# Router bias on TensorE, logits compared in place, expert numbers of the tiles counted among seven

## The reference

```python
xn = layernorm(x)                      # x: 16 x 256 x 128, 4096 tokens in 32 tiles of 128
s = attention(xn)                      # 16 heads of 8, LoRA on q, k, v, ALiBi, causal
logits = xn @ Wr + br                  # 8 experts
indices = argmax(softmax(logits))
for i in range(8):                     # a token not routed to i enters expert i as zeros
    h = relu((xn * (indices == i)) @ W1[i] + b1[i])
    f = f + (h @ W2[i] + b2[i])
out = x + s * silu(f)
```

## Time and profile before

| | us |
|---|---|
| median of 3 runs | 296.31 |
| lowest, highest | 295.81, 296.85 |
| the profiled execution: its own time | 296.07 |
| its span, first to last instruction | 294.2 |
| outside the span | 1.87 |
| PE busy | 267.8 (91%) |
| DVE busy | 228.1 (78%) |
| ACT busy | 185.5 (63%) |
| POOL busy | 152.6 (52%) |

### The profile page before, as it was taken

How to read it: one execution, slowest core, us unless ns; L and a number is a source line. 1 busy time by engine, 2 the same in 40 slices (tenths; PEclk the granted TensorE clock), 3 DMA queues, 4 the chain that set the end, 5 groups by cost and what they waited for, 6 DMA issues and landing times.

```text
span 294.2 us, 12787 instructions
## 1 busy us (share of the span) xinstructions
PE 267.8 (91%) x5196; PEld 203.6 (69%) x5196; DVE 228.1 (78%) x483; ACT 185.5 (63%) x331; POOL 152.6 (52%) x226
## 2 busy tenths in 40 slices
PE   7899999684996999999999999999999999979962
PEld 3556555353674788888887888888788888856641
DVE  3788999789987578596868768685875868676996
ACT  3335355444466668777777778777776876558960
POOL 3073293115436577866677667667766533343100
PEclk9999999979999799999999999999999999999997
DMA  4799556687415442332425433231524623108553
GB/s 137 207 240 212 127 166 194 203 240 225 112 36 134 109 126 67 95 97 57 108 55 129 123 101 84 74 91 51 133 51 96 147 54 90 30 29 250 138 163 111
DMA packets 50970, 35.98 MB, mean 122 GB/s; under 512 B 5112, under 2 KB 48376, under 8 KB 50784
## 3 DMA queue, kind: packets, MB, share of 16 engines
q1 hardware_dynamic: 46680, 28.89, 37.0%
q0 software_dynamic: 2496, 5.12, 7.0%
q10 hardware_dynamic: 1736, 1.15, 1.6%
HBM read 15.28 MB, written 6.75 MB: 75 GB/s over the span
## 4 chain that ended last, share of the span: by engine, by line
PE 68%; DVE 18%; issue 6%; DMA 3%; POOL 2%; SPq 1%; ACT 1%; ACTq 0%; DVEq 0%; POOLq 0%
PE bank L1359 14%; PE bank L1367 12%; PE bank L1273 11%; PE bank L1324 10%; PE bank L1183 4%; DVE row_max L812 4%; PE bank L1281 3%; PE bank L1343 3%; PE bank L1253 2%; PE bank L1190 2%; DVE xn_all L1063 2%; PE bank L1351 2%; DVE w_slots L977 2%; DVE xn_all L1057 1%; DVE o_turned L1020 1%
## 5 line engine op out<-in xcount | busy, mean ns | idle before, releaser
L812 DVE TENSOR_REDUCE row_max<-bank 128x2 f32<-128x512 f32 (+3 forms) x176 | 105.6, 627 | 19.2 <-PE bank L1261 16.3
L757 ACT ACTIVATE probs<-bank 128x512 f32<-128x512 f32 (+1 forms) x176 | 89.5, 558 | 46.4 <-PE bank L1281 46.1
L1273 PE MATMUL bank<-qk_stack 64*64 64x64 bf16 (+3 forms) x1024 | 60.8, 237 | 6.5 <-ACT probs L757 3.3
L1253 PE MATMUL bank<-qk_stack 64*64 64x64 bf16 (+3 forms) x1024 | 61.7, 237 | 1.1 <-DMA qk_stack<-parts 0.7
L554 POOL DMA_INDIRECT expert_rows<-y_slot,token_of x39 | 38.6, 990 | 37.2 <-PE bank L1359 22.8
L532 POOL DMA_INDIRECT xs_slot<-normalised_rows,from_row x39 | 39.7, 1018 | 24.9 <-PE bank L1281 17.9
L1273 PEld LDWEIGHTS bank<-qk_stack 64*64 64x64 bf16 x1024 | 34.3, 108 | 23.6 <-issue 10.7
L739 ACT ACTIVATE w_slots<-w_all 128x1156 f32 x39 | 45.5, 1167 | 4.0 <-issue 3.4
L1324 PE MATMUL bank<-probs,v_diag 128*32 128x64 f32 (+3 forms) x1024 | 46.5, 311 | 1.2 <-issue 1.0
L1045 DVE TENSOR_TENSOR hT<-bank,w_slots 128x512 f32<-128x512 f32 x39 | 27.0, 691 | 23.3 <-PE bank L1359 23.3
L1359 PE MATMUL bank<-xsT_slot,w_slots 128*128 128x128 f32 x312 | 44.6, 286 | 0.2 <-issue 0.2
(11 more groups left out here) (132 smaller groups left out, 346.1 us busy)
## 6 DMA issues: line engine op xcount, KB each, us to landing
qk_stack<-parts SPq DMA_DIRECT2D x120, 64.0 KB, 2.1
qk_stack<-parts SPq DMA_DIRECT2D x32, 128.0 KB, 2.8
w_all<-w_experts SPq DMA_DIRECT2D x8, 512.0 KB, 4.6
x_all<-x SPq DMA_DIRECT2D x7, 512.0 KB, 5.2
normalised_rows<-xn_all SPq DMA_DIRECT2D x4, 512.0 KB, 5.2
xn_all<-expert_rows SPq DMA_DIRECT2D x8, 256.0 KB, 5.2
out<-xn_all SPq DMA_DIRECT2D x7, 256.0 KB, 3.2
xs_slot<-normalised_rows,from_row POOLq DMA_INDIRECT x39, 3.2
```

Source lines behind the costliest of these rows:

```text
L757: act.activation(probs[:, m % PROBS, 0:w], bank[:, 0:w], ACT.Exp).then_inc(emptied, 1)
L812: dve.tensor_reduce(row_max[b % 2][:, n, pairs[0]:pairs[-1] + 1], bank[:, 0:ln_u * len(pairs)].rearrange("p (c k) -> p c k", k=ln_u), AX.X ...
L1253: pe.matmul(bank[to, c * ln_u:(c + 1) * ln_u], q[rows, p, n * BLK:(n + 1) * BLK], k[rows, p, 0:(n + 1) * BLK], start=(c == 0), stop=False, ...
L1273: pe.matmul(bank[rows, c * ln_u:(c + 1) * ln_u], k[rows, p, kb * BLK:(kb + 1) * BLK], q[rows, p, kb * BLK:], start=(c == 0), stop=False, s ...
```

## The change

The bias travels in row 0 of 32 more columns of the array that holds the dense weights (`dense`, 288 KB where it was 272), and its own DMA goes. Behind the four logits matmuls of each `route` PE issues four more, with one row of weights (the bias) and a row of ones as data, 256 columns each, into the same PSUM columns. The wait for the constants moves from DVE to PE. `keep_logits` is the transposition alone; its target is now a part of `xsT_slot`, a buffer not yet in use, with room for all 32 tiles, and `choose` reads 8 of each 32 columns there. The tile's expert number is the count over seven totals, which needs no limit; DVE ends with the sum, and POOL converts it behind `fill_v` at (2, 4).

```diff
-        dense = sb("dense", [P, 4 * P + 32])
+        dense = sb("dense", [P, 4 * P + 64])
+        br_sb = dense[0:1, 4 * P + 32:4 * P + 64]
-        br_sb = sb("br_sb", [P, E])
-        te_cmp = sb("te_cmp", [1, SLOT_TILES, E])
+        te_cmp = sb("te_cmp", [1, SLOT_TILES, E - 1])
+        logits_turned = xsT_slot[:, :, :, :].rearrange("p r j k -> p (r j k)").rearrange("p (n e) -> p n e", e=32)
+        logits = logits_turned[:, :, 0:E]
...
+            def keep_tile_experts():
+                pool.wait_ge(S["tile_sums_done"], 1)
+                pool.tensor_copy(tile_expert[:, :], te_f[:, :]).then_inc(S["tile_expert_done"], 1)
...
                     if i + 1 < NB and g == FILL_V:
                         fill_v(i + 1)
+                    if (i, g) == TILE_EXPERTS_AT:
+                        keep_tile_experts()
...
-            act.dma_start(br_sb[:, :], br.partition_broadcast(P)).then_inc(S["br_in"], 16)
...
-                dve.transpose(logits_turned[:, :, :].rearrange("p n e -> p (n e)"), bank[:, 0:ROUTE_TILES * 32]).then_inc(emptied, 1)
-                wait_vec_emptied(dve, "logits", r)
-                if r == 0:
-                    dve.wait_ge(S["br_in"], 16)
-                    dve.wait_ge(S["constants_in"], 16)
-                dve.tensor_tensor(logits[:, tiles, :], logits_turned[:, :, 0:E],
-                                  br_sb[:, :].unsqueeze(1).to_broadcast([P, ROUTE_TILES, E]), ALU.add).then_inc(S["logits_turned_done"], 1)
+                dve.transpose(logits_turned[:, tiles, :].rearrange("p n e -> p (n e)"), bank[:, 0:ROUTE_TILES * 32]).then_inc(emptied, 1)
...
-                dve.wait_ge(S["logits_turned_done"], ROUTES)
+                for r in range(ROUTES):
+                    wait_vec_emptied(dve, "logits", r)
...
-                te_shape = [1, SLOT_TILES, E]
+                te_shape = [1, SLOT_TILES, E - 1]
...
-                chained(dve.tensor_reduce(te_f[:, 0, :], te_cmp[:, :, :], AX.X, ALU.add), TILE_EXPERTS_AT, 1)
-                then(dve.tensor_scalar(te_f[:, 1, :], te_f[:, 0, :], float(E - 1), None, ALU.min))
-                dve.tensor_copy(tile_expert[:, :], te_f[:, 1, :]).then_inc(S["tile_expert_done"], 1)
+                dve.tensor_reduce(te_f[:, :], te_cmp[:, :, :], AX.X, ALU.add).then_inc(S["tile_sums_done"], 1)
+                maxima_between(*TILE_EXPERTS_AT, 1)
...
+                if r == 0:
+                    pe.wait_ge(S["constants_in"], 16)
                 bank, full = begin_vec("logits", r)
...
                     last = pe.matmul(bank[32 * j:32 * j + 32, 0:ROUTE_TILES * 32].rearrange("p (n t) -> p n t", t=32), wr_sb, tokens[:, j],
-                                     start=True, stop=True, skip_group_check=True)
+                                     start=True, stop=False, skip_group_check=True)
+                for j in range(4):
+                    last = pe.matmul(bank[32 * j:32 * j + 32, 0:ROUTE_TILES * 32].rearrange("p (n t) -> p n t", t=P), br_sb,
+                                     ones_f[0:1, :].unsqueeze(1).to_broadcast([1, 2, P]), start=False, stop=True, skip_group_check=True)
```

## The result

The changed kernel takes **300.25 us** (median of 4, 298.51 to 301.33), the kernel before 296.58 on the same chip; ratio 1.0129, 95% interval 1.0087 to 1.0171. Slower, as forecast, but by 3.7 us and not by 1.8: outside the range. The profiled execution took 298.51 us, its span is 296.7; it is the quickest of the four, so the profile shows 2.4 us of the 3.7.

What follows compares the result with a forecast made beforehand. PE, full from 100 to 240 us, was taken as the bound, so its arrival there counts: 1.78 - 0.25 + 0.30 = +1.83 us, median 298.1 us; own range about 297.4 to 299.3, stretched to other cases without the tails 295.7 to 299.4.

Steps and rivals of the forecast that it cites:

- Four groups, 0.53 each, less 0.34: +1.78.: Bias matmuls in four routes delay PE by 0.53 each; its 0.34 wait at 35.47 absorbs part: +1.78 us at 54.75.
- The addition, -0.25.: On DVE in route 3, removing the bias addition from the path saves 0.25 us; the other three are worth nothing.
- POOL's conversion, +0.30.: On POOL between `fill_v` and the fetch of tile 1, the new conversion costs 0.30 us, bounds 0.1 and 1.2.
- PE's return near 96.5.: After waiting for tile 3's rows, PE would be back at about 96.5 us where it was 94.65.
- whatever comes late at 100 us comes late at the end, and the change touches nothing in it: PE's full stretch from 100 to 240 us: nothing gained or lost there, so PE's arrival delay reaches the end unchanged.
- The matmuls hide: Rival: route 3's 0.89 pause covers added matmuls, +0.94 us; if routes 0 and 1 are covered too, +0.22; chance 0.17.
- The clock stays up: Rival: both falls to 1.2 GHz, from 58.82 and 96.37 us, vanish; the second costs 1.7; total 296.1 us; chance 0.17.
- One after another: Rival: one-row bias matmuls don't run side by side, 2.2 us per route, 6.7 in all, 304.8 us; chance 0.04.
- faster by DVE: Rival: DVE sets the pace in the first 46 us, so its saved work counts: -0.93 us, 295.4; chance 0.08.
- The drain.: In the routes, the step from 128 weight rows to one drains TensorE once more each, 4 x 0.04 = 0.16 us.
- at most 0.04: Around a logits group on PE, a change of matmul shape costs at most 0.04 us.

Runs made afterwards that it cites:

- again2: The changed kernel without further edit, run again beside the kernel before on chip 2: 299.40 us against 295.87, ratio 1.0111.
- after_again3: The changed kernel without further edit, run once more beside the kernel before on chip 4: 299.05 us against 296.50, ratio 1.0108.
- after_split: The changed kernel with 32 `warm` matmuls of 512 columns each written as two of 256 (5260 weight loads): 298.35 us, ratio 1.0061 to the kernel before.
- bf16_int: The changed kernel with the bias as three 16-bit rows, DVE writing the tile sum as whole number, no POOL conversion: 297.61 us, ratio 1.0055 to the kernel before.
- before_split: The kernel before with only 32 `warm` matmuls of 512 columns each written as two of 256 (5228 weight loads): 297.74 us against 296.50, ratio 1.0050.
- no_bias3: The changed kernel without the bias matmuls, bias left out of the logits, on chip 4: 296.79 us against 296.50 for the kernel before, ratio 1.0021.
- double_bias: The changed kernel with four more one-row matmuls per route, a row of zeros as data: 302.13 us, ratio 1.0150 to the kernel before.
- bf16_bias: The changed kernel with the bias split into three 16-bit rows, one 16-bit matmul per group: 297.48 us against 295.87 for the kernel before, ratio 1.0052.

## Why the prediction was right or wrong

- **Four groups, 0.53 each, less 0.34: +1.78.** Right in mechanism: a group takes 0.57, PE's 0.34 wait at 35.47 is gone, and first logits to transposition grew by 1.77 in the profiled execution (33.00 to 31.23) and 1.81 in `again2`. It grew by only 1.27 in `after_again3` and 1.45 in `after_split`: the early pause lies in this stretch and is another length each time, so the agreement to hundredths is luck.
- **The addition, -0.25.** Half right: -0.16. Where one DVE instruction was removed, a gap of 0.13 now stands between the transposition and its reader.
- **POOL's conversion, +0.30.** Right: 0.21 by itself, +0.34 from fetch to fetch (0.32 in `again2`), and `bf16_int`, without it, is back at 6.55.
- **PE's return near 96.5.** It was 96.00, but this kernel began its first logits 0.39 earlier (23.13 for 23.52), which the change doesn't explain; `again2` returned at 97.31, with one more fall of the clock ahead of it, at 74.58 us, where DVE sets the pace.
- **The step that failed: "whatever comes late at 100 us comes late at the end, and the change touches nothing in it".** It holds to tile 38: 142.84 us in the changed kernel and 142.92 in the kernel before from the 5th tile to the 39th. It fails behind it, by +1.0 to +1.3 up to the end of the span. The sum put this term at nothing. The change adds 32 weight loads, and with that count a pause of 0.3 to 0.6 us falls into the values that the last outputs wait for. That it comes with the count is shown by `before_split`, which has it without the change, and `after_split`, which has the change without it. The pause is worth 0.4 to 0.7 of the 1.0 to 1.3; the rest stands where the clock was at 0.50 in the tail. In medians the count costs 1.24 (`before_split`) or 0.70 (`after_again3` over `after_split`). The measured terms of the path are 1.3 to 1.8, - 0.16 and + 0.34, together 1.5 to 2.0; with the count 2.2 to 3.2. The three comparisons on chips without gaps have 2.6, 3.5 and 3.7 (intervals 2.3 to 4.1, 2.6 to 4.0, 2.6 to 5.1 us). What they have above that sum, up to 1 us, stays open; the lower mean clock may be 0.4 to 0.5 of it. The 16-bit kernel leaves a like remainder: it has no pause in the tail, its terms make 0.88 - 0.34 - 0.16 + 0.34 = 0.7, and it measured 1.6 (0.7 to 2.4).
- **"The matmuls hide"** named the right object, the pause of route 3, and the wrong outcome. The pause did move, but only to the values ahead of the logits, so nothing was covered; I looked for what moving it could save and not for what another pause, moved, could cost.
- **"The clock stays up"**: its price of 1.7 was 1.5, but both falls are in the changed kernel's profile. **"One after another"** (0.57 for a group) and **"faster by DVE"** (0.28 slower without any added matmul, `no_bias3`) are out.
- **The drain.** The Trainium skill, TensorEngine Tiling (Array Packing), Key Properties, has a change of tiling mode drain TensorE. The trace agrees, with about 0.1 us for a change of shape: in `double_bias` the first one-row group, with another one-row group behind it, took 0.45 (30.82 to 31.27), the second, with a change of shape behind it, 0.55 (31.27 to 31.82), and the lone one in the changed kernel 0.57. The prediction's "at most 0.04" was too low, but no harm came of it: its 0.53 was read from a group that had such a change behind it, and the four groups came out 4 x 0.04 = 0.16 dearer, as its sentence on the drain has it. The groups differ in more than what follows them, so 0.1 is an estimate.

No version beats the kernel before. Of the complete changed ones on the faster chips `bf16_bias` is the best (1.0052).

## What to carry to other kernels

Where a kernel is PE-bound, compute the price of added matmuls from the like group of the trace, and expect most of it to come through. Then look for pauses in the middle of a line with no semaphore wait at that place: note the number of the instruction at each, and compare before and after. An edit of the number of instructions moves the program past them, and can gain or lose a microsecond far from the edit; to tell that from the edit's own cost, run the old kernel with the same number of instructions added and nothing else.

## What the runs showed of the hardware

- PE's pauses at loads 713 or 714 and 4898 recur across kernels whose lines there differ: the first in all 18 profiles, with 0.2 to 2.1 us of idle time in 17 of them, the second in the four with 5228 loads on the faster chips. That it is the supply of instructions fits, but is argued, not shown.
- Chips differ: medians of the same kernel are 295.9, 296.5, 303.1 and 305.2 us, and the slower two show pauses in the steady stretch. The largest of these sit at places of the program (near load 1647 in kernels with 5196 loads, near 1679 with 5228), not at fixed numbers.
- A matmul with one row of f32 weights costs what one with 128 rows does; the same columns in 16 bits with three rows cost 0.22 and not 0.57 us.
- Two such f32 groups of the same shape in a row start 0.46 us apart; with another shape behind it a group takes 0.54 to 0.57.
- One kernel on the two faster chips takes about 1.4 us more for 0.01 less of mean clock, by that fitted line.
